# A four-layer conditional network on one core: slot reloads, first traces, the rows of 1/std and the last tile in another order

## The chip, the core and the metric

The kernel runs on one core of a Trainium2 chip. The metric is the device time of one execution in microseconds (us); less is better. The engines are PE (TensorE, matmuls), DVE (VectorE), ACT (ScalarE), POOL (GpSimd) and SP (SyncE, which here only issues DMAs); POOL issues DMAs too. Each engine works through its own list in order; semaphores join them.

## What is computed

The input x is 4 sequences of 1024 tokens with 512 features. Four layers are added to it in turn, some with weights picked by an index per sequence:

```
x = x + L0(x)   # gelu MLP, 512 -> 2048 -> 384 shared + 128 of a picked expert
x = x + L1(x)   # picked 512x512 product and bias
x = x + L2(x)   # see below
x = x + L3(x)   # picked 512x512 product and bias

L2:  ctx      = causal_ema(x, tau_ctx)
     wg       = sigmoid([x, ctx] @ Wg.T + bg);  gated = x * wg
     mod      = 0.5 + sigmoid(gelu(x @ Wn1.T + bn1) @ Wn2.T + bn2)       # 4 rows
     temporal = sum over 4 taus of softmax(blend) * causal_ema(gated * mod)
     out      = (gelu(x @ Wsoma.T + bsoma) * sigmoid(temporal @ Wtemp.T + btemp)) @ Wout.T
     result   = (out - mean) / sqrt(var + 1e-5) * gamma + beta
```

causal_ema is h = alpha*h + x over the tokens. Results stay close to fp32: every product is made of three matmuls, high part by high part, high by low, low by high.

## The kernel before, in words

Features lie on the 128 partitions (512 = KC = 4 chunks), tokens along the row, in NT = 8 tiles of TOK = 512 tokens, two per sequence. LAST is tile 7. `split_product` (L891 to L893) issues the three matmuls of one chunk; a 512x512 product of a tile is 4 outputs m by 4 chunks c by 3 = 48 matmuls with 512 columns. All work of PE is fp32 with 4-byte elements.

**First half, layers 0 and 1.** A loop over UNITS = 128 units u = 16 t + j: `fc1(u)` (12 matmuls), `fc2(u - 2)` (12 matmuls), and layer 1 of the tile before (`l1`) in units j = 4 to 7. ACT applies gelu and makes the high part of h, DVE the low part (`h_hl`). x lives in `x_raw`, its two parts in `x_hl`, two buffers each. When x2 = x + L0 + L1 of a tile is ready, x2 goes to `x2_dram` and its two parts to `x2hl_dram`. In the last 16 units layer 2 of tile 0 begins: PE does `n1(0)` at j = 8, `mo(0)` at j = 9, and `gate(0, 0)`, `gate(0, 1)`, `gate(0, 2)` at j = 11, 13, 15; DVE makes the weights `wg_hl`, then the first traces.

**The seam.** After the units PE does `so(0, 0)`, `so(0, 1)`, layer 1 of tile 7, `gate(0, 3)`, `so_pair(0)` and goes into the second half.

**Second half, layers 2 and 3.** Per tile r, PE does: `n1` (12 matmuls), `gate(r, 0)` (24), `mo` (one fp32 product for the four modulation rows), `rb(r - 2)` (spreads 1/std over the partitions by a product with a diagonal matrix), `te(r - 1, .)` (48), `gate(r, 1)`, `gate(r, 2)`, `l3(r - 2, .)` (48), `gate(r, 3)`, `ou(r - 1, .)` (48), `so(r, 0)`, `so(r, 1)`, `ss(r - 1)` (sum of squares over partitions), `so_pair(r)` (outputs 2 and 3 of Wsoma together). The layer input is read from six slots `x2_slot`, each [2 parts, 1 + 512 tokens]; token -1 stands in front, so `gate` reads each chunk twice, at element 1 and at element 0. Slots 0 and 1 of a new tile are free a tile early; slots 2 and 3 only when `so_pair` of the tile before has read its chunks 0 and 1 (`s_x2free`). SP issues the slot loads (L393).

DVE does the traces: per tile and chunk one `scan_g`, `gated_of`, four `drive_of`, four `trace_of` (scans), three `add_of`, cut in `traces_a` to `traces_d`; then the low parts of temporal (`temporal_low`), which `te` waits for. ACT holds the tanh and gelu functions and the high parts. The four rows of mod go over DRAM to all partitions (`mod_dram`, `mod_t`, POOL). Norm of tile i: ACT squares `ou`'s banks, DVE adds them (`sum_squares`), PE `ss`, ACT `rows_std`, DVE `rows_rstd` (reciprocal and four `diag` tiles, L1391), PE `rb`, DVE `z_of`, `x3_of`; `l3` follows.

Engine orders are written out by hand; nothing reorders them. Addresses are set by hand too (`place(name, KiB, shape)`): slots begin at 6 KiB and 112 KiB and are 4128 bytes apart, `l3w_hl[3]` is at 120.0625 KiB.

## Time and profile before

| | |
|---|---|
| median of 3 runs | 1443.73 us (1442.28 to 1444.29) |
| the profiled execution, device time | 1442.82 us |
| its span, first to last instruction | 1441.1 us |
| PE busy | 1379.8 us (96%), 6000 matmul records |
| DVE busy | 758.8 us (53%) |
| ACT busy | 480.6 us (33%) |
| POOL busy | 143.3 us (10%) |
| mean granted TensorE clock | 0.982 of full speed |
| HBM traffic | 67.46 MB read, 33.65 MB written, 70 GB/s |

The device time has 1.7 us around the span. Shares are means over the whole span; the slices of the page show where an engine is not busy.

### The profile page before, as it was taken

The page shows a single profiled execution, that of the slowest core. Times are in us where ns is not written, and L with a number is a line of the kernel's source. Part 1 is how long each engine was busy: PE and PEld are TensorE (multiplying, and loading weights), DVE is VectorE, ACT ScalarE, POOL GpSimd, SP SyncE. Part 2 cuts the span into 40 slices and gives each one's busy share as a digit, 9 for nine tenths or more (in the row PEclk, how much of TensorE's full clock was granted, in tenths as well). Part 3 has the DMA queues.
Part 4 walks back from the last instruction along what each step waited for, and adds up shares of the span by engine and source line. Part 5 has one row for each costly group of instructions (what it writes and reads, how often), then busy time and mean ns, then how long its engine had stood idle before and what let it go on. Part 6 is the DMA issues. An engine that isn't in the chain of part 4 may idle for free.

```text
span 1441.1 us, 15155 instructions
## 1 busy us (share of the span) xinstructions
PE 1379.8 (96%) x6000; PEld 1124.0 (78%) x6000; DVE 758.8 (53%) x1066; ACT 480.6 (33%) x798; POOL 143.3 (10%) x168
## 2 busy tenths in 40 slices
PE   7999999999999999999989959599999999999988
PEld 6888888888888888888867847478787878787876
DVE  3342331322232322313233766979798979897973
ACT  5442331322323313313222312333434343434343
POOL 2000100100001001001002130012101210121000
PEclk9999999999999999999999979799999999999998
DMA  4420500501404105005125362021222122211101
GB/s 126 132 66 15 131 8 8 147 0 51 88 8 120 27 0 132 15 23 124 67 88 118 117 146 103 0 88 59 89 88 89 59 88 88 88 59 59 59 15 44
DMA packets 37419, 102.09 MB, mean 71 GB/s; under 512 B 5556, under 2 KB 9652, under 8 KB 33380
## 3 DMA queue, kind: packets, MB, share of 16 engines
q1 hardware_dynamic: 30468, 77.90, 18.3%
q0 software_dynamic: 6880, 23.23, 5.9%
q8 instruction: 47, 0.77, 0.2%
q14 instruction: 24, 0.20, 0.0%
HBM read 67.46 MB, written 33.65 MB: 70 GB/s over the span
## 4 chain that ended last, share of the span: by engine, by line
PE 88%; DVE 7%; DMA 2%; ACT 2%; issue 1%; SPq 0%; DVEq 0%; ACTq 0%
PE bank L891 29%; PE bank L893 29%; PE bank L892 29%; DVE drive L1325 1%; DMA x_slot<-x2hl_dram 1%; DVE temporal_lo L1151 1%; DVE drive L1312 1%; DVE temporal L1335 1%; PE bank L953 1%; DVE x_hl L1151 1%; DVE temporal L1325 0%; PE bank L1048 0%; DVE l3w_hl L1151 0%; ACT mod_row L645 0%; ACT ts_hi L664 0%
## 5 line engine op out<-in xcount | busy, mean ns | idle before, releaser
L1151 DVE TENSOR_TENSOR h_hl<-bank,h_hl 128x512 fp32r<-128x512 f32 x128 | 88.6, 692 | 544.4 <-ACT h_hl L747 544.4
L891 PE MATMUL bank<-x_hl,wa 128*128 128x512 f32 x512 | 201.1, 393 | 7.7 <-DVE x_hl L1151 7.1
L892 PE MATMUL bank<-x_hl,wa 128*128 128x512 f32 x512 | 200.4, 391 | 0.0
L893 PE MATMUL bank<-x_hl,wa 128*128 128x512 f32 x512 | 200.4, 391 | 0.0
L893 PE MATMUL bank<-h_hl,wa 128*128 128x512 f32 x512 | 199.2, 389 | 0.0
L892 PE MATMUL bank<-h_hl,wa 128*128 128x512 f32 x512 | 199.2, 389 | 0.0
L891 PE MATMUL bank<-h_hl,wa 128*128 128x512 f32 x512 | 199.2, 389 | 0.0
L743 ACT ACTIVATE bank<-bank,small_sb 128x512 f32<-128x512 f32 x128 | 84.6, 661 | 265.1 <-PE bank L893 265.1
L747 ACT ACTIVATE h_hl<-bank 128x512 fp32r<-128x512 f32 x128 | 76.7, 599 | 259.5 <-PE bank L893 259.3
L891 PEld LDWEIGHTS bank<-x_hl,wa 128*128 128x128 f32 x512 | 97.0, 190 | 30.6 <-issue 9.8
L893 PEld LDWEIGHTS bank<-x_hl,wa 128*128 128x128 f32 x512 | 96.8, 189 | 20.4
L892 PEld LDWEIGHTS bank<-x_hl,wa 128*128 128x128 f32 x512 | 96.9, 189 | 20.0
L892 PEld LDWEIGHTS bank<-h_hl,wa 128*128 128x128 f32 x512 | 96.1, 188 | 20.0
L893 PEld LDWEIGHTS bank<-h_hl,wa 128*128 128x128 f32 x512 | 96.1, 188 | 20.0
L891 PEld LDWEIGHTS bank<-h_hl,wa 128*128 128x128 f32 x512 | 96.0, 188 | 19.9
L891 PE MATMUL bank<-x_slot,wg_hl 128*128 128x512 f32 x256 | 101.8, 398 | 0.6 <-DVE wg_hl L1151 0.6
L893 PE MATMUL bank<-x_slot,wg_hl 128*128 128x512 f32 x256 | 101.9, 398 | 0.0
L892 PE MATMUL bank<-x_slot,wg_hl 128*128 128x512 f32 x256 | 101.4, 396 | 0.0
L1312 DVE SCALAR_TENSOR_TENSOR drive<-gated,small_sb,mod_t 128x512 f32<-128x512 f32 x128 | 92.0, 740 | 8.3 <-DMA mod_t<-mod_dram 6.2
L525 POOL DMA_DIRECT2D x2hl_dram<-x_hl x28 | 21.1, 768 | 709.8 <-DVE x_hl L1151 709.8
L1335 DVE TENSOR_TENSOR temporal<-drive,temporal 128x512 f32<-128x512 f32 x96 | 66.0, 688 | 1.1
L1151 DVE TENSOR_TENSOR x_hl<-x_raw,x_hl 128x512 fp32r<-128x512 f32 x96 | 61.7, 684 | 1.9 <-ACT x_hl L623 1.9
(147 smaller groups left out, 2334.5 us busy)
## 6 DMA issues: line engine op xcount, KB each, us to landing
x_slot<-x2hl_dram SPq DMA_DIRECT2D x32, 513.0 KB, 4.4
x2hl_dram<-x_hl POOLq DMA_DIRECT2D x28, 512.0 KB, 10.0
x_dram<-x_raw SPq DMA_DIRECT2D x8, 1024.0 KB, 5.4
xt<-x_dram SPq DMA_DIRECT2D x8, 1024.0 KB, 6.0
mod_t<-mod_dram POOLq DMA_DIRECT2D x8, 1024.0 KB, 5.0
x_raw<-in_x SPq DMA_DIRECT2D x7, 1024.0 KB, 10.3
out<-y_sb SPq DMA_DIRECT2D x28, 256.0 KB, 2.3
stage<-in_l_w SPq DMA_DIRECT2D x16, 256.0 KB, 3.1
```

The lines of the kernel that those rows point to most:

```text
L525: eng.dma_start(x2hl_dram[t, c, :, :, 1:1 + TOK], x_hl[t % 2][:, :, c, :].bitcast(F32)).then_inc(s_hlst[c], 16)
L743: eng.activation(ps[:, :], ps[:, :], ACT.Gelu, bias=fc1_b_sb[:, j:j + 1]).then_inc(s_gelu, 1)
L747: eng.activation(h_hl[u % 2][:, 0, :], ps[:, :], ACT.Copy).then_inc(s_hhi, 1)
L891: eng.matmul(ps, w_hi, x_hi, start=first, stop=False)
L892: eng.matmul(ps, w_hi, x_lo, start=False, stop=False)
L893: return eng.matmul(ps, w_lo, x_hi, start=False, stop=final)
L953: eng.matmul(mo_bank(i)[0:TAUS, :], wn2_sb, h1[:, :], start=True, stop=True).then_inc(s_pe["MO"], 1)
L1151: return eng.tensor_tensor(lo, raw, hi.bitcast(F32), ALU.subtract)
L1312: eng.scalar_tensor_tensor(drive[d % 2][:, :], gated[:, :], blend_sb[:, TAUS * c + d:TAUS * c + d + 1], mod_t[:, d, :], ALU.mult, ALU.mult ...
L1325: eng.tensor_tensor_scan(traced, alpha[:, 1 + d:2 + d].to_broadcast([P, TOK]), drive[d % 2][:, :], start, ALU.mult, ALU.add).then_inc(s_tr ...
L1335: eng.tensor_tensor(temporal[:, c, :], drive[d % 2][:, :], temporal[:, c, :], ALU.add).then_inc(s_add, 1)
```

## The change

- **Seam, PE.** `l1(LAST, .)` is split: outputs 0 and 1 before `gate(0, 3)` and `so_pair(0)`, outputs 2 and 3 behind them, in banks 4 and 5. `gate(1, 1)` comes ahead of `te(0, .)`.
- **Seam, SP.** The loads of slots 2 and 3 of tile 1 are issued ahead of the last `store_x2` and of the last store of x2's two parts.
- **Seam, ACT and DVE.** `h1_of(0)`, `mod_of(0)` stand ahead of the high parts of x2; first traces of tile 0 go into other units; the parts of x2 of tile 7 are made behind `temporal_low(0)`.
- **1/std.** For tiles 0 to 6 the row of 1/std goes to DRAM and back to all partitions (`spread_rstd`, SP), and `rb` and the `diag` tiles remain for tile 7 alone. `norm_of` stands ahead of `scan_g(r, 0)`; `gate(r, 2)` no longer waits for z.
- **Last tile.** PE's order of `l3(6, .)`, `ou(7, .)`, `ss(7)`, `rb(7)` changes; squares go to SBUF tiles and stand ahead of the copies; the last two low parts of spikes are made one by one; x3's high part goes to `ts_hi`; a small Sqrt stands ahead of `y_of(6, 0)`.
- **Slots.** A slot row is 8 + 512 elements, token 0 at element 8; slots are 4160 bytes apart; `l3w_hl[3]` is at 120.125 KiB.

```diff
@@ places
-        SLOT_KIB = (2 * (1 + TOK) * 4 + 31) // 32 * 32 / KIB
-        x2_slot = [place(..., [2, 1 + TOK], F32R)
+        LEAD = 8
+        SLOT_KIB = 2 * (LEAD + TOK) * 4 / KIB
+        x2_slot = [place(..., [2, LEAD + TOK], F32R)
-        l3w_at = (152, 156, 200, 120.0625)
+        l3w_at = (152, 156, 200, 120.125)
+        rstd_t = nc.alloc_sbuf_tensor_at("rstd_t", [P, TOK], F32, offset=constants_at[0] - 4 * TOK)
-            return bank[6 + m % 2] if t < LAST else bank[m]
+            return bank[6 + m % 2] if t < LAST else bank[(0, 1, 4, 5)[m]]
+        last_squares = (sumsq, drive[0], drive[1], gated)
@@ SP
-                eng.dma_start(x2_slot[s][:, :, :].bitcast(F32), x2hl_dram[i, c]).then_inc(s_slot[s], 16)
+                eng.dma_start(x2_slot[s][:, :, LEAD - 1:].bitcast(F32), x2hl_dram[i, c]).then_inc(s_slot[s], 16)
+            def spread_rstd(i):
+                on.wait_ge(s_rstd, i + 1)
+                eng.dma_start(rstd_dram[i].rearrange("(q p) -> p q", p=P), rstd[:, :],
+                              allow_slow_non_contiguous=True).then_inc(s_rst, 16)
+                on.wait_ge(s_rst, 16 * (i + 1))
+                on.wait_ge(s_z, KC * i)
+                eng.dma_start(rstd_t[:, :], rstd_dram[i:i + 1, :].to_broadcast([P, TOK])).then_inc(s_rld, 16)
...
                 if r + 1 < NT:
                     load_slot(r + 1, 2)
                     load_slot(r + 1, 3)
+                if r < NT:
+                    spread_rstd(r - 1)
@@ ACT
+                if t == LAST and j == 9:
+                    h1_of(0)
+                if t == LAST and j == 10:
+                    mod_of(0)
                 if t and j in (X2_UNIT, X2_UNIT + 1):
                     x2_hi(t - 1, 2 * (j - X2_UNIT))
...
             for m in range(KC):
                 spikes_hi(LAST, m)
+
+            on.wait_ge(s_rstd, LAST)
+            on.wait_ge(s_rst, 16 * LAST)
+            eng.activation(std[:, 0:1], eps_sb[:, 0:1], ACT.Sqrt).then_inc(s_chain, 1)
             y_of(LAST - 1, 0)
-            y_of(LAST - 1, 1)
             for m in range(KC):
                 o_of(LAST, m)
+            y_of(LAST - 1, 1)
+            rows_std(LAST)
             y_of(LAST - 1, 2)
-            rows_std(LAST)
-            y_of(LAST - 1, 3)
             for m in range(KC):
                 x3_hi_of(LAST, m)
+            y_of(LAST - 1, 3)
@@ PE
             def n1(i):
-                if i:
+                if i > 1:
                     on.wait_ge(s_soma, KC * (i - 1) + 2)
                 else:
-                    on.wait_ge(s_x2, KC * (LAST - 1) + 3)
+                    on.wait_ge(s_x2, KC * NT if i else KC * (LAST - 1) + 3)
...
             so(0, 1)
-            for m in range(KC):
-                l1(LAST, m)
+            l1(LAST, 0)
+            l1(LAST, 1)
             gate(0, 3)
             so_pair(0)
+            l1(LAST, 2)
+            l1(LAST, 3)
             for r in range(1, NT):
                 n1(r)
                 gate(r, 0)
                 mo(r)
-                if r > 1:
-                    rb(r - 2)
+                if r == 1:
+                    gate(r, 1)
                 for m in range(KC):
                     te(r - 1, m)
-                gate(r, 1)
+                if r > 1:
+                    gate(r, 1)
...
-            rb(LAST - 1)
             for m in range(KC):
                 te(LAST, m)
             l3(LAST - 1, 0)
-            l3(LAST - 1, 1)
             for m in range(KC):
                 ou(LAST, m)
+            l3(LAST - 1, 1)
+            ss(LAST)
             l3(LAST - 1, 2)
-            ss(LAST)
+            rb(LAST)
             l3(LAST - 1, 3)
-            rb(LAST)
@@ DVE
             def rows_rstd(i):
                 on.wait_ge(s_std, i + 1)
+                on.wait_ge(s_rst, 16 * i)
                 eng.reciprocal(rstd[:, :], std[:, :]).then_inc(s_rstd, 1)
+                if i < LAST:
+                    return
...
             for r in range(2, NT):
+                norm_of(r - 2)
                 scan_g(r, 0)
-                norm_of(r - 2)
                 traces_a(r, 0)
```

How it moves instructions, at three places. On ACT, in units j = 9 and 10 of tile 7 (`h_68` is h1, `x_hl_50` takes the high part of x2, `wg_hl` a weight), before:

```order
L747 ACTIVATE h_hl_55<-bank 128x512 [waits s_fc2,s_gelu]
L633 ACTIVATE x_hl_50<-x_raw_52 128x512 [waits s_pe_L1,s_x2]
L633 ACTIVATE x_hl_50<-x_raw_52 128x512 [waits s_x2]
L567 ACTIVATE wg_hl<-stage_58 128x512 [waits s_st1,s_wgp]
L567 ACTIVATE wg_hl<-stage_57 128x512 [waits s_st0]
L641 ACTIVATE h_68<-bank,small_sb 128x512 [waits s_pe_N1]
```

and now:

```order
L775 ACTIVATE h_hl_55<-bank 128x512 [waits s_fc2,s_gelu]
L662 ACTIVATE h_68<-bank,small_sb 128x512 [waits s_pe_N1]
L654 ACTIVATE x_hl_50<-x_raw_52 128x512 [waits s_pe_L1,s_x2]
L654 ACTIVATE x_hl_50<-x_raw_52 128x512 [waits s_x2]
L588 ACTIVATE wg_hl<-stage_58 128x512 [waits s_st1,s_wgp]
L588 ACTIVATE wg_hl<-stage_57 128x512 [waits s_st0]
```

h1, which `mo(0)` waits for, has moved ahead of four operations, two of which wait for DVE.

On SP at the seam (`x_slot_70` and `x_slot_71` are chunks 2 and 3 of tile 1), before:

```order
L393 DMA x_slot_75<-x2hl_dram 128x1026 [waits s_halo1,s_hlst1]
L346 DMA stage_58<-in_wout 128x512 [waits s_stlo]
L346 DMA stage_57<-in_wout 128x512 [waits s_stlo]
L360 DMA x_dram<-x_raw_53 128x2048 [waits s_x2]
L461 DMA x2hl_dram<-x_hl_51 256x1x512 [waits s_x2lo] x4
L393 DMA x_slot_70<-x2hl_dram 128x1026 [waits s_halo2,s_hlst2,s_x2free]
L393 DMA x_slot_71<-x2hl_dram 128x1026 [waits s_halo3,s_hlst3,s_x2free]
```

and now:

```order
L405 DMA x_slot_75<-x2hl_dram 128x2x513 [waits s_halo1,s_hlst1]
L405 DMA x_slot_70<-x2hl_dram 128x2x513 [waits s_halo2,s_hlst2,s_x2free]
L405 DMA x_slot_71<-x2hl_dram 128x2x513 [waits s_halo3,s_hlst3,s_x2free]
L358 DMA stage_58<-in_wout 128x512 [waits s_stlo]
L358 DMA stage_57<-in_wout 128x512 [waits s_stlo]
L372 DMA x_dram<-x_raw_53 128x2048 [waits s_x2]
L482 DMA x2hl_dram<-x_hl_51 256x1x512 [waits s_x2lo] x4
```

The two reloads have passed four stores of 512 KB and one of 1 MB, and a load has two pieces per partition (2x513) where it had one (1026).

On DVE at the seam (L1250 adds layer 1 of tile 7 into x2; L1151 and L1288 are a low part and the scan of `scan_g`), before:

```order
L1288 SCALAR_TENSOR_TENSOR bank<-alpha,bank 128x512 [waits s_pe_WG]
L1250 SCALAR_TENSOR_TENSOR x_raw_53<-bank,l_b_sb,x_raw_53 128x512 [waits s_pe_L1] x4
L1296 SCALAR_TENSOR_TENSOR gated<-bank,xt_91 128x512 [waits s_wgt]
...
L1335 TENSOR_TENSOR temporal<-drive_78,temporal 128x512 [waits s_tracel,s_trace]
L1151 TENSOR_TENSOR x_hl_51<-x_raw_53,x_hl_51 128x512 [waits s_x2hi] x4
L1288 SCALAR_TENSOR_TENSOR bank<-alpha,bank 128x512 [waits s_pe_WG]
```

and now:

```order
L1368 TENSOR_TENSOR temporal<-drive_77,temporal 128x512 [waits s_trace]
L1283 SCALAR_TENSOR_TENSOR x_raw_53<-bank,l_b_sb,x_raw_53 128x512 [waits s_pe_L1] x2
L1358 SCALAR_TENSOR_TENSOR drive_78<-alpha,drive_78 128x512 [waits s_drive]
L1368 TENSOR_TENSOR temporal<-drive_78,temporal 128x512 [waits s_add,s_trace]
L1283 SCALAR_TENSOR_TENSOR x_raw_53<-bank,l_b_sb,x_raw_53 128x512 [waits s_pe_L1] x2
L1321 SCALAR_TENSOR_TENSOR bank<-alpha,bank 128x512 [waits s_pe_WG]
```

All of chunk 2 of tile 0 now stands ahead of the last two additions, and the low parts of x2 of tile 7 have left this place.

## Rows read from the trace of the kernel before

**Rows 1.** Waits of PE, longest first: total us, times, longest us

```profile
PE bank L1048 <- DVE sumsq L1381: 17.3, 1, 17.3
PE bank L891 <- DMA x_slot<-x2hl_dram: 15.1, 1, 15.1
...
PE bank L891 <- DVE temporal_lo L1151: 5.7, 2, 3.2
PE bank L953 <- ACT h L641: 5.6, 1, 5.6
PE bank L891 <- DVE x_lo L1151: 3.0, 1, 3.0
```

**Rows 2.** Timeline of ACT around mo(0): start, us, operation

```profile
748.52 0.60 ACT L747 ACTIVATE h_hl<-bank 128x512 fp32r<-128x512 f32 x1 [2.12 <-PE bank L893]
...
753.25 0.67 ACT L641 ACTIVATE h<-bank,small_sb 128x512 f32<-128x512 f32 x1
```

**Rows 3.** Stretches: us, busy of PE, PEld, DVE, ACT, POOL; PEclk, DMA, GB/s

```profile
753.97:757.16 3.19, 3.19 (x6) 1.25 (x6) 0.18 (x1) 0.00 (x0) 0.00 (x0) 0.51 1.24 140
806.90:840.59 33.69, 33.53 (x145) 27.07 (x144) 30.93 (x43) 9.05 (x18) 9.93 (x6) 1.00 0.42 148
857.21:866.99 9.78, 9.78 (x31) 7.37 (x31) 0.00 (x0) 0.69 (x1) 0.00 (x0) 0.71 0.27 111
915.45:932.97 17.52, 0.17 (x2) 0.04 (x1) 17.21 (x27) 9.64 (x16) 0.00 (x0) 0.66 0.00 0
```

**Rows 4.** The chain at the seam and at mo(4): start, us, what

```profile
840.12 17.05 DMA x_slot<-x2hl_dram
...
1095.69 0.96 PE bank L953 x2
...
1097.98 1.24 DVE temporal_lo L1151
```

**Rows 5.** One stretch, columns as in Rows 3: the traces of chunk 3 of tile 0 on DVE

```profile
843.55:853.61 10.06, 0.00 (x0) 0.00 (x0) 9.91 (x13) 0.00 (x0) 4.31 (x5) 0.61 1.04 110
```

**Rows 6.** DMA issues: KB each, median us from issue to landing

```profile
x_slot<-x2hl_dram SPq DMA_DIRECT2D x32, 513.0 KB, 4.4
...
mod_t<-mod_dram POOLq DMA_DIRECT2D x8, 1024.0 KB, 5.0
...
mod_dram<-mod_row POOLq DMA_DIRECT2D x8, 8.0 KB, 1.8
```

**Rows 7.** The load of slot chunk 3 of tile 5 alone, issued at 1157.2 us

```profile
DMA to landing us min/median/max: 4.2/4.2/4.2
```

**Rows 8.** Timeline of PE: in l3(0, 0), then n1(5) at its chunk 3

```profile
976.19 0.39 PE L891 MATMUL bank<-x_hi,l3w_hl 128*128 128x512 f32 x1
...
976.87 0.40 PE L891 MATMUL bank<-x_hi,l3w_hl 128*128 128x512 f32 x1
...
977.57 0.39 PE L891 MATMUL bank<-x_hi,l3w_hl 128*128 128x512 f32 x1
...
1161.90 0.40 PE L891 MATMUL bank<-x_slot,wn_hl 128*128 128x512 f32 x1
```

**Rows 9.** Stretches of 48 matmuls: gate(2, .), l3(0, .), ou(7, .)

```profile
963.63:974.83 11.20, 11.20 (x50) 9.05 (x49) 11.17 (x15) 3.07 (x5) 4.19 (x4) 1.00 0.00 0
974.83:985.83 11.00, 11.00 (x50) 9.02 (x48) 9.92 (x11) 2.79 (x5) 3.17 (x2) 1.00 0.20 73
...
1402.21:1413.10 10.89, 10.89 (x50) 9.01 (x48) 1.38 (x2) 4.25 (x7) 0.00 (x0) 1.00 0.06 24
```

**Rows 10.** Stretches of the last tile: before te(7, .), and in l3(7, .)

```profile
1377.70:1383.24 5.54, 1.29 (x9) 0.99 (x9) 5.47 (x12) 3.07 (x6) 0.00 (x0) 0.86 0.00 0
...
1423.58:1429.29 5.71, 5.71 (x14) 4.45 (x14) 4.94 (x8) 1.89 (x3) 0.00 (x0) 0.50 0.00 0
```

**Rows 11.** Timeline of DVE in the last tile

```profile
1379.17 0.88 DVE L1391 TENSOR_SCALAR diag<-ident,rstd 128x128 f32<-128x128 f32 x4
...
1398.74 2.36 DVE L1151 TENSOR_TENSOR spikes_lo<-soma,ts_hi 128x1024 fp32r<-128x1024 f32 x2 [0.44 <-ACT ts_hi L675]
```

More of the change, by code:

```diff
@@ L453, in _ @@
             load_xt(1)
-            load_slot(1, 0)
-            load_slot(1, 1)
+            for c in range(KC):
+                load_slot(1, c)
             load_plain(OU_NO, wout[:, 0, :])
@@ L800, in _ @@
             wtemp_hi(3)
-            wg_tanh(0, 2)
-            for c in range(KC):
-                x2_hi(LAST, c)
-            wg_tanh(0, 3)
             soma_of(0, 2)
             soma_of(0, 3)
+            wg_tanh(0, 3)
             h1_of(1)
@@ L810, in _ @@
                 temporal_hi(0, m)
+            for c in range(KC):
+                x2_hi(LAST, c)
             wg_tanh(1, 0)
@@ L1492, in _ @@
                 x1_lo(LAST, c)
[L1493 to L1494 removed]
             wtemp_lo(2)
             wtemp_lo(3)
[L1497 to L1499 removed]
             traces_a(0, 2)
             traces_b(0, 2)
[L1502 to L1503 removed]
+            traces_c(0, 2)
+            x2_of(LAST, 0)
+            x2_of(LAST, 1)
+            traces_d(0, 2)
+            x2_of(LAST, 2)
+            x2_of(LAST, 3)
             scan_g(0, 3)
[L1505 to L1506 removed]
             traces_a(0, 3)
@@ L1511, in _ @@
             temporal_low(0)
+            for c in range(KC):
+                x2_lo(LAST, c)
             scan_g(1, 0)
```

129 lines of the change are left out of this document (68 added, 61 removed).

## The prediction

> **What bounds the kernel now.** I read the page, then PE's waits, then stretches of the trace around each wait, then the chain of waits. The page has PE busy for 1379.8 of 1441.1 us, in each of its matmuls; only idle time of PE and matmuls that run slow can be won. PE's waits are few and long [rows 1]: 17.3 us for DVE's sums of squares, 15.1 for a slot reload, 5.7 in two places for temporal_lo, 5.6 for h1 and 3.0 for the last tile's x_lo. After a long one the granted clock stays at 0.5, which is 1.2 GHz, for some matmuls: 14 records of l3(7) take 5.71 us [rows 10] where the clean pace, 10.89 us for 48 [rows 9], gives 3.2. So a wait costs more than its length. From tile 2 to tile 6 PE has no wait that is listed; there the change can win little. All sums are against the profiled execution's 1442.82 us, which is 0.9 below the median of the three runs, 1443.73. Less than 0.2% (2.9 us) counts as no change.
>
> **h1 ahead on ACT.** In unit 9 of tile 7 ACT starts its h_hl operation at 748.52 and h1 only at 753.25, behind two high parts of x2 and two of wg, which wait for DVE [rows 2]. Put directly behind h_hl, h1 starts near 749.0, takes 0.67, and mo(0) starts near 749.8 in place of 753.97: -4.2 us. The stretch behind it ran at clock 0.51, 3.19 us [rows 3]; mo's 0.96 [rows 4] and three matmuls at 0.23 are 1.65: -1.5 if the wait that is left, 1.5 us, brings no fall of the clock. The moved mod_of(0) now stands ahead of the last wg parts on ACT, so gate(0, 0) waits some 0.6 longer. Together -5.1.
>
> **Slot reloads ahead.** PE waits 15.1 us because the reload stands on SP behind the last stores and then shares the DMA engines with them: 17.05 us from issue to landing [rows 1, 4], against a median of 4.4 [rows 6]. Now the loads are issued when so_pair(0) has read its first chunks, and the rest of so_pair (4.2 us), l1's two outputs (24 matmuls, 5.45 us) and n1's first chunks lie over them: some 11 us cover for 4.4. The wait goes. So does the slow stretch behind it: 31 records in 9.78 us [rows 3], 7.2 at the pace of the slots (11.20 for 48 [rows 9]): -2.6. SP now blocks on s_x2free ahead of the loads of Wout; these are used some 30 us later.
>
> **What is late next at the seam.** DVE is busy for 30.93 of 33.69 us from 806.90 on [rows 3], so PE, 5.1 us earlier, catches up with it. l1(LAST, 0) needs all low parts of x1, and DVE does more traces ahead of them: I put the wait at 1.3 us in place of 0.4: +0.9 (bounds 0 and 3). n1(1) now waits for the addition of layer 1's last output (bank 5): +1.0. From the end of l1(LAST, 3), PE needs that 1.0, n1 2.8, gate(1, 0) 5.6, mo 1.0, a wait of 0.7 for mod_of(1), gate(1, 1) 5.6: 16.7 us to te(0). DVE needs two additions 1.5, a scan and tanh 2.2, the traces of one chunk 10.06 [rows 5] and high and low parts of temporal 2.5: 16.3 us. They come out level, PE a hair behind, so the wait for temporal_lo, 3.2 us [rows 1], goes and 0.7 stands in its place: -2.5.
>
> **gate(1, 1) ahead of te(0).** It covers that wait, but DVE's way to ss(0) begins with te(0)'s end: tanh, spikes, Wout's parts, then three chunks of traces ahead of sum_squares. In the long wait before ss(0) DVE is busy for 17.21 of 17.52 us [rows 3]: DVE is the bound there, with the same work in the same order in both kernels. Whatever te(0) gives, ss(0) gives: gate(1, 1)'s 5.6 us are lost to it, and PE's wait grows from 17.3 to about 22. To ss(0), then: -5.1 - 15.1 - 2.6 + 0.9 + 1.0 - 2.5 + 5.6 = -17.8.
>
> **1/std over DRAM.** It takes rb from PE, 0.9 us a tile. But te's third chunk waits for temporal_lo, and that chain hangs on mo: mo from 1095.69 for 0.96, tanh, the high part, temporal_lo from 1097.98 for 1.24 [rows 4]: 2.6 us behind mo. rb and six matmuls of te lay over it; without rb PE waits 1.2 us where it waited 0.3. Tiles 1 to 6: 0. The row of 1/std itself needs a store and a broadcast: 1.8 + 5.0 us by the rows of mod, which moves four times as much [rows 6]; it has some 14 us, and x3 has another 9 before l3 reads it. scan_g behind norm_of costs DVE 1 us a tile for an uncovered tanh, the four diag tiles give back 0.8; DVE waits for temporal_lo's input each tile anyway: 0. At the end of tile 7, where DVE is busy for 5.47 of 5.54 us [rows 10], the diag tiles (0.8 us between their neighbours, [rows 11]) do count: -0.8.
>
> **Last tile.** spikes_lo's first pair starts at 1398.74 and needs half of 2.36 [rows 11]: ou(7) can start at 1400.0, behind one output of l3(6), in place of 1402.21: -2.2. From ou's end to l3(7) there lay 10.5 us: l3, ss, l3, rb and a wait of 3.0 for x_lo [rows 1]. Now l3(6, 3) lies over that chain: two outputs 5.5, ss 0.8, rb 0.9, chain 3.0: 10.2, so -0.3, of which PE idles some 0.3 only. The early Sqrt takes the table load off the way, but an output of l3 covers that way already: 0. With PE nearly unbroken the slow stretch goes: -2.5. Together -5.0.
>
> **Rows at 32 bytes.** 48 matmuls on slots take 11.20 us, on other tiles 10.89 [rows 9]: 6.5 ns each, 8 us over the 1248 of them. l3 takes 11.00, and its chunk 3 takes 0.70 us where chunk 2 takes 0.68, with more behind it [rows 8]. Only its weights differ: they lie at an odd multiple of 64 bytes. So 64 bytes are not enough, 32 neither, and I give the slots 0; l3w_hl[3] moves to a multiple of 128: 8 x 0.11 = -0.9. The Trainium skill (SBUF - State Buffer, "Operand start alignment") asks only that an operand start at a multiple of its element's size, and says that this is legality, not speed; taken as no effect at all it would make this term 0. The trace does not agree: the two paces above differ. Bounds: 0, and -5.6 if 32 bytes do it (rival below).
>
> **A load in two pieces.** Chunk 3 of tile 5 lands 4.2 us behind its issue, at 1161.4 [rows 7]; PE uses it at 1161.90 [rows 8]: 0.5 us to spare, in six tiles. 256 pieces of 2 KB in place of 128 of 4 KB: no row has such a load. Lower bound no later; upper bound 1.5 us later (6 x 1.0 = +6). mod_t with twice the bytes lands in 5.0, 0.8 later than 4.2 [rows 6, 7]; I take a little under that: +0.5 in all.
>
> **Sum.** -17.8 - 0.8 - 5.0 - 0.9 + 0.5 = -24.0: 1418.8 us, 1419.5 beside the median. I say 1419.
>
> **Rivals.**
> - **DVE or the slots late** (0.14). The seam's levelled chains slip by 2 to 4 us, or the pieces land late by their upper bound. For it: DVE is full at the seam. Against: both chains came out equal from rows, with slack at h_lo. +4 to +7: 1423 to 1426.
> - **32 bytes do it** (0.07). 864 of the 1248 matmuls get the clean pace: 1413.5. Against it: the weights at 64 bytes.
> - **The clock falls at the small waits** (0.06). I leave some twelve waits of 0.3 to 1.5 us: four at the seam, one in each of six tiles where 0.3 becomes 1.2, two in the last tile. The shortest known fall costs 1.5 us (1.65 became 3.19, less its wait), the others 2.5. Ten falls at 1.5 make 1434; from ten at 2.5 on the gain is gone, and twelve at 2.6 to 2.8 are 31 to 34 us: 1450, slower than before. Against it: no listed wait under 3 us shows a fall, and the six waits of 0.3 show none. The Trainium skill (TensorE: Matmul & The Clock Gate, "A second HAM failure mode: psum-queue depth-cycling") says that short idling between groups of matmuls, often enough, makes the clock swing to and fro. Whether waits of 1.2 us in 72 are such, no row shows.
> - **The seam gains less than it says** (0.05): the reload is early but n1 meets another late chunk, PE keeps 5 to 10 us and the slow stretch: 1426 to 1431.
>
> **How the numbers follow.** The forecast has 0.68, its own range 1415 to 1423. With the 32-byte case below and the late case above, 1412 to 1427 leaves out less than 2 in 10. Faster by over 0.2%: all but the deep clock case: 0.95. Same 0.02, slower 0.03.
>
> **What would show it.** Right: PE waits for h1 about 1.5 us; no wait for x_slot at n1(1); te(0) near 853; the wait for sumsq at 20 us or more; te's wait in each tile near 1.2; clock 1.00 throughout l3(7); slots still at 11.2 for 48 and l3 at 10.9. Wrong: a wait for x_slot in the tiles, a fall of the clock inside tiles 2 to 6, ss(0) later than 917, or gates at 10.9.

## The result and the profile after

The changed kernel takes **1471.45 us** (1469.48 to 1474.66) beside 1443.01 us (1442.23 to 1444.29) for the kernel before: a ratio of 1.0198, 95% interval 1.0176 to 1.0221. It is 2% slower; the forecast was 1419 us, with 0.95 on faster. The profiled execution has a span of 1467.8 us.

From the page of the changed kernel: busy times, DMA packets, and the chain that ended last.

```profile
PE 1380.8 (94%) x5944; PEld 1120.5 (76%) x5944; DVE 754.0 (51%) x1039; ACT 475.7 (32%) x799; POOL 138.4 (9%) x168
...
DMA packets 46218, 103.93 MB, mean 71 GB/s; under 512 B 9364, under 2 KB 13460, under 8 KB 42180
...
PE 64%; DVE 20%; DMA 9%; issue 4%; ACT 2%; POOL 0%; SPq 0%; DVEq 0%; ACTq 0%; POOLq 0%
```

PE works as long as before. The chain has DVE and DMA in it for 29%, so PE waits for them. The waits of the changed kernel in the seam (735 to 940 us), as in [rows 1]:

```profile
PE bank L1082 <- DVE sumsq L1414: 19.8, 1, 19.8
...
DVE drive L1345 <- DMA mod_t<-mod_dram: 9.2, 1, 9.2
...
PE bank L925 <- DVE wg_hl L1184: 6.6, 1, 6.6
PE bank L925 <- DVE spikes_lo L1184: 6.4, 1, 6.4
```

and in the tiles and the tail (940 to 1440 us):

```profile
DVE o_sb L1435 <- DMA rstd_t<-rstd_dram: 28.5, 5, 10.5
...
PE bank L925 <- DMA x_slot<-x2hl_dram: 14.1, 3, 7.8
PE bank L925 <- DVE temporal_lo L1184: 11.1, 7, 4.9
...
PE bank L925 <- ACT y_sb L758: 8.4, 6, 2.5
...
PE bank L925 <- DVE x_lo L1184: 5.0, 1, 5.0
```

The 15.1 us of [rows 1] at n1(1) are gone. New are waits for slots inside the tiles, for y_sb in l3 and, on DVE, for the row of 1/std. The matmuls of mo mark the tiles; of each kernel the first and last start between 900 and 1400 us, before and after. Each mo is two matmuls 0.4 us apart, so these are the first of mo(2) and the second of mo(7); the table goes by the first of each.

```profile
L953 PE MATMUL bank<-h,small_sb x12: 592/592/593, 950.4 to 1314.0; 128*4 128x512 f32 x12
```

```profile
L990 PE MATMUL bank<-h,small_sb x12: 592/592/593, 944.1 to 1339.5; 128*4 128x512 f32 x12
```

| stretch, us | before | forecast | after | difference |
|---|---|---|---|---|
| start to mo(2) | 950.4 | 932.6 | 944.1 | -6.3 |
| mo(2) to mo(7), five tiles | 363.2 | 363.2 | 395.0 | +31.8 |
| mo(7) to the last matmul | 123.6 | 117.8 | 124.7 | +1.1 |

The forecasts are the prediction's sums for the seam and the tail; its two small terms for the tiles, -0.9 and +0.5, are left out. So 11.5 us are missing at the seam, 31.8 were lost in the tiles, and the tail gave nothing.

**The tiles.** The DMA rows of the changed kernel, beside [rows 6]:

```profile
x_slot<-x2hl_dram SPq DMA_DIRECT2D x32, 513.0 KB, 5.6
...
mod_t<-mod_dram POOLq DMA_DIRECT2D x8, 1024.0 KB, 4.9
...
rstd_t<-rstd_dram SPq DMA_DIRECT2D x7, 256.0 KB, 5.3
...
mod_dram<-mod_row POOLq DMA_DIRECT2D x8, 8.0 KB, 5.5
...
rstd_dram<-rstd SPq DMA_DIRECT2D x7, 2.0 KB, 9.6
```

The store of 2 KB takes 9.6 us, where I gave it the 1.8 of mod's 8 KB; that one moves rows of 2048 bytes, this one 512 numbers of 4 bytes, each a piece of its own: the page counts 9364 packets under 512 bytes where that of the kernel before has 5556, and seven stores of 512 pieces are 3584 of the 3808 more. Even mod's store now takes 5.5. SP's queue around it in tile 5, and the last chunk's load, issued 1.7 us ahead of the store (its view alone, as in [rows 7]):

```profile
1157.96 1.92 SPq L405 DMA_DIRECT2D x_slot<-x2hl_dram  x2
1161.04 0.38 SPq L424 DMA_DIRECT2D rstd_dram<-rstd  x1
1170.66 0.33 SPq L428 DMA_DIRECT2D rstd_t<-rstd_dram  x1
1171.40 1.19 SPq L405 DMA_DIRECT2D x_slot<-x2hl_dram  x2
```

```profile
  PE bank L925: 5.7, 1
...
DMA to landing us min/median/max: 10.5/10.5/10.5
```

Before, it landed after 4.2 us. SP is blocked from 1161 to 1171, and the next tile's chunks 0 and 1 leave 10 us behind the store, where before they left with the other two. The same load took 12.6 us in tile 7, where the store came 1.7 us behind it too, and 4.7 to 5.4 in the tiles where it came 3.2 us or more behind. The distance alone does not decide it: in tile 2 the store came 0.6 us behind, and the load landed after 3.8. The chain from tile 4 to tile 5 has both ways in which the row costs:

```profile
1087.28 9.37 DMA rstd_dram<-rstd
1096.67 5.34 DMA rstd_t<-rstd_dram
1102.03 2.74 DVE o_sb L1435 x4
...
1128.26 0.69 ACT y_sb L758
...
1159.36 10.49 DMA x_slot<-x2hl_dram
```

The row is there 14.7 us behind the store's issue, and DVE has waited 6.6 us for it. z, x3, the low parts and all of DVE's queue behind them are late; ACT, which empties the banks of l3 into y_sb, waits for DVE in turn, and l3 waits for its banks. In the next tile the slot is late.

### The profile page after: what moved, and what is told of

It reads as the page before. It is cut to its first block, busy times and chain, and to the rows that moved or that the text cites. A ratio compares the mean times of both kernels' runs of the same rounds, so it can differ in the third digit from the quotient of the medians.

```text
span 1467.8 us, 15032 instructions
## 1 busy us (share of the span) xinstructions
PE 1380.8 (94%) x5944; PEld 1120.5 (76%) x5944; DVE 754.0 (51%) x1039; ACT 475.7 (32%) x799; POOL 138.4 (9%) x168
## 2 busy tenths in 40 slices
DMA packets 46218, 103.93 MB, mean 71 GB/s; under 512 B 9364, under 2 KB 13460, under 8 KB 42180
## 4 chain that ended last, share of the span: by engine, by line
PE 64%; DVE 20%; DMA 9%; issue 4%; ACT 2%; POOL 0%; SPq 0%; DVEq 0%; ACTq 0%; POOLq 0%
PE bank L925 21%; PE bank L926 21%; PE bank L927 21%; DVE drive L1358 5%; DMA rstd_dram<-rstd 3%; DVE temporal L1368 2%; DMA x_slot<-x2hl_dram 2%; DVE drive L1345 2%; DVE temporal L1358 2%; DMA rstd_t<-rstd_dram 2%; DVE bank L1321 1%; DMA mod_t<-mod_dram 1%; DVE o_sb L1435 1%; DVE spikes_lo L1184 1%; DVE xt L1441 1%
## 5 line engine op out<-in xcount | busy, mean ns | idle before, releaser
L925 PEld LDWEIGHTS bank<-x_slot,wg_hl 128*128 128x128 f32 x256 | 49.5, 193 | 20.3 <-issue 7.0
## 6 DMA issues: line engine op xcount, KB each, us to landing
x2hl_dram<-x_hl POOLq DMA_DIRECT2D x28, 512.0 KB, 10.5
```

What stands on the lines that cost most here:

```text
L925: eng.matmul(ps, w_hi, x_hi, start=first, stop=False)
```

## The experiments

All times are medians beside the kernel before on the same chip; us between two kernels are the difference of their ratios times 1442.7.

**1/std back on PE, the layout back, and both.** `rb_back` restores diag, rb and the order of scan_g; `layout_back` has LEAD = 1 and the old places; `both_back` is seam and tail alone.

```diff
-                if r < NT:
-                    spread_rstd(r - 1)
+                if r > 1:
+                    rb(r - 2)
```

> The changed kernel with 1/std on PE again, as in the kernel before: diag tiles on DVE and rb on PE for all eight tiles, no store and no broadcast of the row, scan_g(r, 0) ahead of norm_of again; seam, tail and slot rows stay changed. Theory S (the store of the row, 512 pieces of 4 bytes, takes 9.6 us where I gave it 1.8; it makes z, x3 and l3 late, and it crowds the load of the slot's last chunk): from mo(2) to mo(7) 5 x 72.6 = 363 us in place of 395.0, and the tail loses its two waits, 6 us more: 1430 us, 1426 to 1435, no n1 waits of 8 and 10 us. Rival P (the slot loads in two pieces per row are late by themselves): only the waits of l3 go, n1 still waits about 8 us in two tiles, 1450 to 1456. Rival C (the small waits of te pull the clock down): the waits of te go back to 0.3 us, and the rest of the loss with them, but the slots land as late as now.

> The changed kernel with the slot rows as before: one column of lead, one piece of 4104 bytes per partition, and gated, drive, sumsq, l3w_hl[3] and y_sb0 at their old places; 1/std still goes over DRAM. Theory S: the store of the row still takes some 10 us and the l3 waits stay, 1460 to 1472; the slots' matmuls at 6.5 ns above the clean pace as before, l3's chunk 3 slower by 0.02 us per three matmuls. Rival P: the loads land within 4.5 us again and n1 has no wait, 1440 to 1446.

> The changed kernel with both the rows of 1/std and the slot layout as before: what is left is the seam and the tail. Theory S: within 5 us of the run with only 1/std back, so 1426 to 1436. The difference between the two is the price of the layout: by the row of mod_t I gave +0.5 for two pieces and -0.9 for l3w, so the two agree within 1 us. Rival P: this one is the faster by 10 us or more.

Measured: `rb_back` 1429.92, ratio 0.9915 (0.9898 to 0.9931); `layout_back` 1447.19, 1.0037 (1.0008 to 1.0065); `both_back` 1429.21, 0.9913 (0.9895 to 0.9931). The row over DRAM costs 41 us. Theory S gave `rb_back` to the microsecond. It did not foresee `layout_back`: beside the small store the old layout is worth 23 us (its six executions lie between 1439.5 and 1453.2), without it nothing. In the trace of `layout_back` no slot is late; the row comes 12.8 to 14.8 us behind its store, and the five tiles take 370.7 us.

**The same row with large pieces.** `cheap_store` stores 4 rows of the identity matrix in place of the row of 1/std, whose values it leaves out for tiles 0 to 6.

```diff
-                eng.dma_start(rstd_dram[i].rearrange("(q p) -> p q", p=P), rstd[:, :],
-                              allow_slow_non_contiguous=True).then_inc(s_rst, 16)
+                eng.dma_start(rstd_dram[i].rearrange("(q p) -> q p", p=P), ident[0:TOK // P, :]
+                              ).then_inc(s_rst, 16)
```

> The changed kernel with one edit: the store to the DRAM row takes 4 rows of 128 numbers of the identity matrix, 4 pieces of 512 bytes, in place of the 512 numbers of 1/std in pieces of 4 bytes. It leaves out the values of 1/std for tiles 0 to 6; every wait, the queue and the broadcast stay. Theory S: the store lands within 2 us, the row is there 7 us after the store's issue, no l3 waits and no long wait of n1: tiles of 72.7, total 1429 to 1435. Rival W (the round trip over DRAM as such, SP blocked in it, and the broadcast's 256 KB crowd the loads): waits of several us stay in l3 and n1, 1445 or more. Rival P (the slots in two pieces): n1 still waits about 8 us in two tiles, 1450 to 1456.

Measured: 1429.32, ratio 0.9907 (0.989 to 0.9925), as `rb_back`. The round trip, its place on SP and the broadcast cost nothing; the 4-byte pieces do all of it. te waits 1.0 us a tile here and rb takes 0.9 in `rb_back`: what I called even is even.

With the row in time, this trace also shows when DVE wants it, that is, how much cover it has. In tiles 2, 3, 5 and 7 z starts 12.9 to 14.1 us behind the store's issue, in tiles 4 and 6 only 10, and in the last tile DVE wants the row after 4. The stores on SP in tile 4 and in the last tile:

```profile
1086.40 0.28 SPq L424 DMA_DIRECT2D rstd_dram<-ident  x1
...
1376.09 0.27 SPq L424 DMA_DIRECT2D rstd_dram<-ident  x1
```

and z there on DVE (x4, its four outputs):

```profile
1096.33 2.73 DVE L1435 SCALAR_TENSOR_TENSOR o_sb<-o_sb,small_sb,rstd_t 128x512 f32<-128x512 f32 x4
...
1380.58 2.74 DVE L1435 SCALAR_TENSOR_TENSOR o_sb<-o_sb,small_sb,rstd_t 128x512 f32<-128x512 f32 x4 [0.35 <-DMA rstd_t<-rstd_dram]
```

**Crowding without lateness: the small store, read by nobody.** `store_unread` adds it to `rb_back`, `unread_one_piece` to `both_back`.

```diff
+                if r < NT:
+                    store_rstd(r - 1)
```

> The run with 1/std back on PE, plus the store of 1/std in 512 pieces of 4 bytes on SP at its place in the changed kernel, which nothing reads and nobody waits for but the next tile's reciprocal and the kernel's end. It tells the crowding apart from the lateness of the row. Theory S, crowding: here the store is issued about 1 us behind the load of the slot's last chunk in every tile (in the changed kernel 1.7 us in the two tiles where that load took 10.5 and 12.6 us, 3.2 us and more in the others, where it took 4.8 to 5.4), so the load lands 6 to 8 us late in six tiles: n1 waits in each, tiles of 78 to 82 us, 1465 to 1485. Rival L (only the lateness of the row costs; the two late loads had another cause): 1430 to 1433.

> The run with the unread 4-byte store (1441.9 us), with the slot layout of the kernel before: one piece of 4104 bytes. Theory T: the load of the last chunk lands within 5.5 us in every tile, no wait of n1 of more than 1 us, 1429 to 1432, so that the whole 12 us of the unread store were its meeting with the loads in two pieces. Rival (the store crowds whatever follows it, the loads of the next tile, mod_t, the results): 1436 or more.

Measured: 1441.92, ratio 0.9998 (0.998 to 1.0017), and 1436.71, 0.9958 (0.9944 to 0.9972). So 12 us against `rb_back`, less than I expected: only one tile of six has the long wait, since after it PE and with it the loads run late, and the store no longer falls just behind them. Some 3 of the 12 us arise at the seam, ahead of the first small store: ss(0) comes at 928.4 where `rb_back` has 925.4. The long wait:

```profile
PE bank L920 <- DMA x_slot<-x2hl_dram: 4.8, 1, 4.8
```

In the second run the last chunk lands after 4.5 us or less in every tile, as theory T said. The total has the rival's number, 6 us above `both_back`, but does not speak for it: ss(0), ahead of the first small store, is already 5.8 us later than in `both_back` (929.2 and 923.4), and so is the landing of mod_t for tile 1 (875.7 and 869.8). From ss(0) to the end the two differ by 1.8 us, and `store_unread` and `rb_back` by 9.0. So most of the cost of the unread store hangs on the loads in two pieces, as T has it. The loads of the next tile's chunks 0 and 1, issued behind the store, land after 10.1 to 15.1 us in both runs, and nobody waits for them. Why mod_t lands late at the seam is open.

**Lateness without small pieces.** `late_row` issues the store of large pieces four times in a chain, `late_row_8` eight times; both leave out the values of 1/std for tiles 0 to 6.

```diff
+                for k in range(4):
+                    eng.dma_start(rstd_dram[i].rearrange("(q p) -> q p", p=P), ident[0:TOK // P, :]
+                                  ).then_inc(s_rst, 16)
+                    on.wait_ge(s_rst, 16 * (4 * i + k + 1))
```

> The changed kernel with the store of 4 pieces of 512 bytes (rows of the identity matrix, so the values of 1/std are left out for tiles 0 to 6) issued and waited for four times over. The row then comes some 6 to 8 us later than in the run with one such store (1429.3 us), about as late as in the changed kernel, but with 28 KB less than nothing to move: lateness without the 512 small pieces. Theory L+C (the 41.5 us between the changed kernel and the run with 1/std on PE are 12 of crowding, as the unread store showed, and the rest lateness): l3 waits of 1 to 6 us in several tiles, 1440 to 1460. Rival (lateness alone is covered, it hurts only where the small pieces also hold the loads up): 1429 to 1434.

> As the run with four large stores in a chain (1429.7 us, the row there 10.8 us behind the first store, and no wait for it), with eight of them: the row 15 to 16 us behind, which is where the changed kernel has it (15.2 to 16.7 us), and still no small pieces. The values of 1/std are left out for tiles 0 to 6. Theory L2 (my cover of 14 us was right, and what lies beyond it is paid: DVE waits for the row, l3 waits behind it, and the last tile loses its start): 1434 to 1455, DVE waits of 2 to 6 us a tile. Rival C2 (only with the small pieces in the queues does it cost; lateness at this size is covered too): 1429 to 1432.

Measured: 1429.73, ratio 0.9914 (0.9897 to 0.993), and 1445.83, 1.0026 (1.0009 to 1.0043). DVE's wait for the row in the one and in the other, 940 to 1440 us:

```profile
DVE o_sb L1436 <- DMA rstd_t<-rstd_dram: 3.8, 1, 3.8
```

```profile
DVE o_sb L1436 <- DMA rstd_t<-rstd_dram: 22.7, 7, 8.2
...
PE bank L926 <- ACT y_sb L759: 5.2, 3, 2.5
```

In `late_row` the row lands 7.9 to 10.8 us behind its first store. That is covered in all tiles but the last, and there it costs nothing either; the theory that expected 1440 us or more is refuted. In `late_row_8` it lands 12.4 to 15.1 us behind, earlier than I expected, and costs 16 us in all; DVE waits in every tile, longest where `cheap_store` shows the shortest cover (4.2 and 4.9 us in tiles 4 and 6, 8.2 in the last). So my cover of 14 us was right for the best tiles only. The run is not wholly free of crowding: mod's store has a median of 3.6 us in it, in place of 1.8. Against `rb_back` the traces split the loss as follows:

| us | seam | five tiles | tail | all |
|---|---|---|---|---|
| row 12.4 to 15.1 us behind its store (`late_row_8`) | 0.5 | 7.9 | 6.8 | 15.1 |
| small store unread (`store_unread`) | 2.2 | 9.7 | 0.2 | 12.0 |
| the changed kernel, row 14.6 to 16.8 us behind | 0.2 | 32.4 | 6.8 | 39.4 |

The tail's loss is lateness alone. In the tiles some 8 us are lateness: `layout_back`, whose slots are in time, loses 8.1 there too. 15 of the 32 us are in neither run; as the row of `late_row_8` is 1 to 3 us earlier than that of the changed kernel, a part of the 15 may be lateness too. The trace shows one sequence twice: l3 stalls for its late row (6 us at 1122, 5 us at 1281, slow matmuls included), the slot loads, which hang on PE, come later, the row, which hangs on DVE, does not, and it falls 1.7 us behind the load of the last chunk, for which n1 then stalls. So two tiles are 14 and 15 us too long, and the others 1.4 at most.

**One piece at the new addresses.** `after_one_piece` is the changed kernel with rows of 520 columns in DRAM too.

```diff
-    x2hl_dram = nc.dram_tensor("x2hl_dram", [NT, KC, P, 2, 1 + TOK], F32, kind="Internal").ap()
+    x2hl_dram = nc.dram_tensor("x2hl_dram", [NT, KC, P, 2, 8 + TOK], F32, kind="Internal").ap()
```

> The changed kernel, 1/std still over DRAM, with rows of 8 + 512 columns in DRAM too, so that a slot's two rows come in one piece of 4160 bytes per partition (128 pieces) where the changed kernel has 256 of 2052 bytes; the halo is stored in pieces of 32 bytes. The rows stay at multiples of 32 bytes. Putting the whole layout back took 24 us off beside this store (1447.2 against 1471.5), and nothing without it (1429.2 against 1429.9). Theory T (the number of pieces is what matters: 256 pieces are not through the queues when the store's 512 pieces come in, 128 are): 1440 to 1450, n1 without a wait of several us, l3 still waiting for its row. Rival A (the addresses, or the other tiles that moved with the layout): 1465 or more, n1 still waits 8 us in some tiles.

Measured: 1443.3, ratio 0.9996 (0.9978 to 1.0015). The slots' addresses are those of the changed kernel; not they, but the pieces, or the rows in DRAM that changed with them (below), cost the 29 us. By the traces 9 of them are won at the seam (mo(2) at 935.0 in place of 944.1), where Wg's load now lands early (below), and 16 in the tiles. The slot is late in one tile still, 8.1 us behind its issue, again with the small store 1.7 us behind it; in tile 5, at the same distance, it lands after 4.9.

**The seam.** `hl7_later` moves the stores of x_hl of tile 7 behind the last loads of Wout; `hl7_h1` also puts h1 back; `hl7_g11` instead puts gate(1, 1) back behind te(0); `best_seam` is `hl7_h1` with xt(2) later too. All have 1/std on PE.

```diff
-            for c in range(KC):
-                on.wait_ge(s_x2lo, KC * LAST + c + 1)
-                eng.dma_start(x2hl_dram[LAST, c, :, :, 1:1 + TOK], ...
             load_xt(2)
             load_plain(OU_NO + 2, wout[:, 2, :])
             load_plain(OU_NO + 3, wout[:, 3, :])
+            for c in range(KC):
+                on.wait_ge(s_x2lo, KC * LAST + c + 1)
+                eng.dma_start(x2hl_dram[LAST, c, :, :, 1:1 + TOK], ...
```

> The run with 1/std back on PE (1429.9 us), and the four stores of x_hl of tile 7, 2 MB in all, on SP behind the last loads of Wout instead of ahead of the load of xt(2). Theory M (the seam fell short of its forecast because the 1 MB broadcast of mod_t for tile 1, issued at 860.6, shares the DMA engines with these stores, issued at 859.0 to 861.2; it lands after 10.8 us in place of 4.4, and DVE waits 9.2 us for it at 863.4): mod_t lands in 5 to 7 us, DVE's wait falls to 2 to 5 us, ss(0) comes 4 to 7 us earlier, 1423 to 1426 us. Rival X (xt(2), 1 MB issued at 862.6, is enough to keep it late): DVE still waits 7 us or more, 1428 or more. Rival Q (DVE's wait for mod_t is covered by its waits for Wout or for PE's gates): the wait goes, ss(0) stays where it is, 1429 to 1431.

> The run before this one, with h1 and mod of tile 0 again behind the high parts of x2 and Wg on ACT, as in the kernel before. Theory W (gate(0, 0) waits for Wg's last part, whose load lands at 763.8 in both kernels, so that PE only waits 6.6 us there instead of ahead of mo(0), and pays the slow stretch there): within 1.5 us of the run before this one, mo(0) near 753.5 and gate(0, 0) where it was. My prediction's step (h1 ahead is worth 5.1 us, and nothing behind it takes that back): 5 us slower, or less where DVE bounds the seam.

> The run with the stores later, and gate(1, 1) behind the four outputs of te(0) again, as in the kernel before. My prediction's step (DVE's way to ss(0) begins with te(0)'s end, so gate(1, 1) ahead of it costs its 5.6 us): ss(0) comes 3 to 5.6 us earlier, with PE waiting 2 to 4 us for temporal_lo ahead of te(0); 1418 to 1423 us. Rival (DVE is bound by its own queue from temporal_low(0) on, and te(0)'s end comes before DVE asks for it): ss(0) stays within 1 us, total within 1.5 us of the run with the stores later, or up to 2 us slower by the clock behind PE's new wait.

> The run with 1/std on PE, the stores of x_hl of tile 7 later and h1 at its old place (1425.3 us), and the load of xt(2), 1 MB, behind the last loads of Wout too. Theory D (ss(0) comes 53.5 us of full DVE behind the landing of mod_t for tile 1: 53.4 to 53.7 in five traces; mod_t still takes 7.6 us there because xt(2) runs beside it): mod_t lands 4.4 to 5.5 us behind its issue near 859.4, DVE waits 1.5 us or less, ss(0) near 918 in place of 920.4, 1422 to 1424. Rival (something else is late next on DVE: Wout's loads, te(0)'s outputs): mod_t is early but ss(0) stays, 1425 to 1426.

Measured: `hl7_later` 1426.59, ratio 0.9887 (0.987 to 0.9903); `hl7_h1` 1425.32, 0.988 (0.9864 to 0.9897); `hl7_g11` 1425.28, 0.9883 (0.9866 to 0.99); `best_seam` 1423.72, 0.9871 (0.9855 to 0.9888). The stores held mod_t up: 4 us. h1 ahead is worth nothing here. gate(1, 1) shows nothing either: ss(0) comes 2.3 us earlier without it, but so does mod_t, which lands at 866.5 in place of 868.8. xt(2) later gives 1.3 us at most, within the intervals: mod_t lands 1.9 us earlier (865.1 in place of 867.0), but ss(0) stays (920.6 and 920.4), because DVE now waits 2.1 us for the high part of Wout (`wout_hl`). That is the rival's reading, not theory D's. The load of mod_t for tile 1, in the kernel before, in the changed one, and in `best_h1` (below):

```profile
DMA to landing us min/median/max: 5.0/5.0/5.0
```

```profile
  DVE drive L1345: 9.2, 1
...
DMA to landing us min/median/max: 12.0/12.0/12.0
```

```profile
  DVE drive L1340: 1.8, 1
...
DMA to landing us min/median/max: 4.6/4.6/4.6
```

**The seam with slot rows in one piece.** `best_one_piece` is `best_seam` with rows of 520 columns; `best_h1` has h1 ahead again; `best_h1_g11` also gate(1, 1) back behind te(0); `halo_4_bytes` is `best_h1` with the halo (the one column of the tile before) in pieces of 4 bytes again. The store of the halo in the changed kernel and in `best_one_piece`:

```diff
-                        eng.dma_start(x2hl_dram[t + 1, c, :, :, 0:1], x_hl[t % 2][:, :, c, TOK - 1:TOK].bitcast(F32),
+                        eng.dma_start(x2hl_dram[t + 1, c, :, :, 0:8], x_hl[t % 2][:, :, c, TOK - 8:TOK].bitcast(F32),
```

> The run before this one, with the slot rows in one piece of 4160 bytes (rows of 520 columns in DRAM, halo in pieces of 32 bytes) at their multiples of 32 bytes. The last chunk then lands as in the kernel before, 4.2 us or less behind its issue, and the 7 small waits of n1 of 0.1 to 0.4 us go; the tile stays at 72.35 us against 72.67 with the old layout if it is the 32 bytes that gave 0.3 a tile. 1 to 2 us faster than the run before: 1421 to 1423. Rival (two pieces cost nothing here, the 0.3 a tile came from them): tiles of 72.6, 1424 or more.

> The run with the slot rows in one piece (1423.65 us), with h1 and mod of tile 0 ahead on ACT again, as in the changed kernel. There the halo goes to DRAM in pieces of 32 bytes, not 4, and Wg's last part lands 4.4 to 4.9 us behind its issue in both runs that have it so, against 8.0 to 13.1 in the eleven others. Theory H (h1 ahead was worth nothing because Wg's late part took its place, and that part was late for the halo's 4-byte pieces): gate(0, 0) starts near 763 in place of 768, PE is 4 to 5 us earlier down to mo(1), ss(0) 3 to 5 us earlier: 1419 to 1421. Rival W2 (some other part is late next, or DVE has it anyway): 1423 to 1424.5.

> The run before this one, with gate(1, 1) behind te(0) again. My prediction's step: 3 to 5.6 us faster by an earlier ss(0). Theory D (ss(0) hangs on the landing of mod_t for tile 1, that is on mo(1), and 53.5 to 55.5 us of DVE behind it; te(0) is in time either way): within 1 us of the run before this one.

> The run with h1 ahead, the slots in one piece and the seam's loads reordered (1418.3 us), with only the halo stored in pieces of 4 bytes again (256 pieces for each of four chunks; the padding of the odd tiles is zeroed once at the start). Theory H: Wg's last part, issued near 754.6, lands 8 us or more behind it, as in the fourteen traces with such a halo (7.8 to 13.1), in place of 4.4 to 4.9; PE waits for gate(0, 0) and has a slow stretch there, 1421 to 1426. Rival (it was the row length in DRAM or the slot loads that made Wg's load early): it lands within 5 us, 1418 to 1419.5.

Measured: 1423.65, ratio 0.9874 (0.9858 to 0.989); **1418.29, 0.9832 (0.9816 to 0.9849)**; 1417.67, 0.9826 (0.981 to 0.9843); 1418.92, 0.9842 (0.9817 to 0.9867). Here h1 ahead is worth 6 us by the ratios and 4.6 by the two traces: Wg's last part is early, and gate(0, 0) follows in time. I had blamed the halo's small pieces for its lateness; `halo_4_bytes` shows that they are not the cause, for Wg's last part lands there after 3.3 to 3.6 us. Nor are the slot loads in two pieces, as it is late in `both_back` too (8.2 us). What is left is the rows in DRAM. With them the large stores change, the 512 KB of x_hl, first in `rb_back`, then in `best_h1`:

```profile
x2hl_dram<-x_hl POOLq DMA_DIRECT2D x28, 512.0 KB, 9.1
```

```profile
x2hl_dram<-x_hl POOLq DMA_DIRECT2D x28, 512.0 KB, 5.7
```

The pieces are as many and as long (2048 bytes). What differs is where they start in DRAM. Rows of 513 columns are 2052 bytes apart, so the starts walk through all multiples of 4, and seven in eight lie off a multiple of 32; in rows of 520 columns all lie on one. Two of these stores are in the queues ahead of Wg's last part. That they hold it up is inferred; no run moved the stores alone. Its load in the changed kernel and in `best_h1`:

```profile
DMA to landing us min/median/max: 10.4/10.5/10.7
```

```profile
DMA to landing us min/median/max: 4.3/4.3/4.4
```

**l3w_hl[3] alone moved by 64 bytes.** `l3w_alone` is `both_back` with this edit; a single execution, 1434.08 us. It is 5 us above `both_back`, and so is its ss(0) (929.0 and 923.4), with mod_t for tile 1 at 875.5 in place of 869.8; so only the pace of l3 is read from it.

```diff
-        l3w_at = (152, 156, 200, 120.0625)
+        l3w_at = (152, 156, 200, 120.125)
```

> The run with seam and tail alone (1429.2 us), with only l3w_hl[3] and y_sb0 moved by 64 bytes to a multiple of 128. My prediction's step: the 48 matmuls of l3 take 10.9 us in place of 11.0, that is 0.11 less a tile, with the third product of each triple at the pace of the others. Theory N (the address is not the cause; with it moved the third product has a median of 396 ns, and 392 at the old place, and 48 take 10.87 against 10.79): l3 0.05 to 0.1 us slower a tile.

The third product of the triples in l3, all four chunks together, before and with l3w_hl[3] at a multiple of 128 (ns, least, median, most):

```profile
L893 PE MATMUL bank<-x_hi,l3w_hl x64: 388/392/398, 1047.9 to 1276.2; 128*128 128x512 f32 x64
```

```profile
L912 PE MATMUL bank<-x_hi,l3w_hl x64: 388/396/398, 1043.9 to 1272.4; 128*128 128x512 f32 x64
```

It got slower, not faster: 48 matmuls of l3 take 11.05 to 11.11 us here, and 11.00 to 11.05 in `both_back`.

## Why the prediction was wrong

**The step that failed** is "1.8 + 5.0 us by the rows of mod, which moves four times as much; it has some 14 us". I priced the store by its bytes. The store measured 9.6 us and the broadcast 5.3 (medians), together 14.6 to 16.8 us for the seven rows, where I had 6.8. The cover was too large as well: 12.9 to 14.1 us in four tiles, 10 in two and 4 in the last. So DVE waited 2.7 to 6.6 us in four tiles and 10.5 in the last. The price decides: `cheap_store`, with 4 pieces in place of 512, has the row after 4.5 to 7.9 us, waits 0.35 us for it once, and comes out at 1429.3, the whole of the 41 us better. The Trainium skill (DMA: Bandwidth & Descriptors, "Rules for kernel authors") says that a strided last dimension becomes one descriptor per element and should be rearranged, and ("Specifications") that pieces under 512 bytes make the DMA engines read, modify and write. The trace agrees with the first: 3808 more packets under 512 bytes, and 9.6 us for 512 pieces of 4 bytes against 1.8 us for 8 KB in large ones [rows 6]. Whether the engines read and modify here, no run shows. Even by my own rows a bound from above was due here: I gave this cost none, though no row of before had such a store. I took the term at 0 and looked for no DMA behind which it stood or which stood beside it.

**A load in two pieces**, bounds 0 and +6, taken as +0.5: alone it costs nothing (`rb_back` and `both_back`, `best_seam` and `best_one_piece` differ by 0.4 us or less). Beside the small store the layout costs 23 us. I priced two edits each by itself, and they share SP's queue, issued 1.7 us apart in the two tiles that lost most.

**h1 ahead**, -5.1: mo(0) came at 748.5, 5.4 us earlier. Then PE waited 6.6 us for wg_hl: Wg's last part landed at 763.8 us, as late as before (763.2), and now nothing covered it. I had looked at ACT's queue behind the moved step, not at the load that gate(0, 0) needs. With that load early, `best_h1` against `best_one_piece`, the step is worth 4.6 to 6 us: the size was right, the cover was not named.

**Slot reloads ahead**, -15.1 - 2.6, x1's low parts and n1(1)'s wait: right. No wait for x_slot at n1(1); te(0) started at 859.6 in place of 853.4; gate(0, 0) had started 4.2 us later than forecast and lost 2.1 more in slow matmuls, which is that difference. In `best_h1` te(0) starts at 853.5.

**ss(0)**: "DVE is the bound there" was right (DVE is busy for 19.79 of the 20.10 us before it), but "DVE's way to ss(0) begins with te(0)'s end" was wrong. It begins with mod_t for tile 1: ss(0) came 53 to 56 us behind its landing in every trace, 53.7 in the changed kernel and 55.3 before. mod_t came 12.0 us behind its issue, and not 5.0, because the stores of x_hl of tile 7 and the load of xt(2) were now issued beside it: 11.2 us in `rb_back`, 7.4 with the stores later, 5.1 with xt(2) later too. So ss(0) came at 926.3 in place of 915.2. And gate(1, 1) ahead of te(0), +5.6, cost nothing that can be told from no change (1418.3 and 1417.7): ss(0) came 0.9 us earlier without it. A grain of my step is left there: with mod_t early DVE also waits for `wout_hl`, 2.7 us with gate(1, 1) ahead and 1.1 without. With mod_t early, gate(1, 1) where the change has it, and Wg early, ss(0) stands at 915.1. That it meets my number is partly luck: te(0) was right, the way from there was not.

**rb for a wait of te**, 0, and te's wait near 1.2: right (1.0 us).

**The tail**, -5.0: right, and hidden. From mo(7) to the last matmul `rb_back` has 118.0 us against 123.6, -5.6, with the diag tiles back. The -0.8 for those tiles is not seen: `cheap_store`, without them, has 118.1. In the changed kernel z of tile 6 waits 10.5 us for its row, and PE waits 5.0 us for x_lo behind it, at a clock of 0.53 for some 4 us. Its wait of 4.9 us for temporal_lo is none of the loss: `cheap_store` has it too, in a tail of 118.1 us.

**Rows at 32 bytes**, slots 0 and l3w -0.9: both wrong, both small. l3's third product went from 392 to 396 ns with l3w_hl[3] at a multiple of 128. The slots' matmuls became faster by 2 to 4 ns (in tile 4 the 72 of gate have means of 392 to 393 ns in `rb_back` and 394 to 396 in `both_back`). From mo(2) to mo(7) that is 362.6 against 363.2 us: 0.1 a tile, not the 0.7 of the rival "32 bytes do it" (5.6 us over eight tiles). I had read an address rule out of one pair of rows that differed in more than the address.

**The rivals.** None named a late row. "DVE or the slots late" had the right engines and 4 to 7 us. The rival of the small waits fell: in `cheap_store` waits of 1.0 us in each of five tiles leave the clock at 1.00. But my argument against it, "no listed wait under 3 us shows a fall", misread the trace: the shorter of the two waits for temporal_lo in [rows 1] is 2.5 us long, and in the 4.8 us behind it (1383.2 to 1388.0) the clock is 0.50. The 0.03 on slower was too little for a change that puts a new store, a wait on SP and a broadcast into every tile of a kernel in which PE waits for nothing there. And a small slip in the last sum: 1443.73 less 24.0 is 1419.7, not 1419.5.

**With the causes mended** (1/std on PE, DRAM rows of 520 columns, the seam's stores and xt(2) later) the rest of the change gives 1418.3 us, or 1417.7 with gate(1, 1) back, 1.7% less than before.

## What to carry to other kernels

Price a DMA by the number and size of its pieces, not by its bytes, and where no row has such pieces, put an upper bound in the range. Read the cover in the tile where it is shortest. Then ask what stands within a few microseconds of it on the same queue. When a step makes an engine earlier, list every input of the next step with its landing time; a load that landed in time before is the next wait. And look for where a busy engine's way begins (here one broadcast, 53 us ahead), not only at its last link.
